# Second layer's product by one level of Strassen's algorithm, with operands of the second batch and the residual kept in HBM

## What is computed

```python
def _L0_xattn_ref(x1, x2, x1_scale, x1_zp, x2_scale, x2_zp):
    q1 = fake_quant(x1, x1_scale, x1_zp)      # clip(round(x / s + z), 0, 255), then (q - z) * s
    q2 = fake_quant(x2, x2_scale, x2_zp)
    return jnp.matmul(q1, q2)

def _L0_ffn_ref(x, W_base, b_base, W_router, lora_A, lora_B):
    logits = xf @ W_router.T
    probs = jax.nn.softmax(logits, axis=-1)
    topk_p, topk_i = jax.lax.top_k(probs, TOP_K)            # 2 of 8 experts
    topk_p = topk_p / jnp.sum(topk_p, axis=-1, keepdims=True)
    w = jnp.sum(jax.nn.one_hot(topk_i, n_experts, dtype=xf.dtype) * topk_p[..., None], axis=1)
    h = jnp.einsum('td,erd->ter', xf, lora_A)
    lora_out = jnp.einsum('ter,eor,te->to', h, lora_B, w) * SCALING
    base = x @ W_base.T + b_base
    return base + lora_out.reshape(x.shape[:-1] + (W_base.shape[0],))

x = x + _L0_xattn_ref(_layernorm(x, axis=-1), ctx_4096, ...)
x = x + _L0_ffn_ref(_layernorm(x, axis=-1), ...)
```

## Time and profile before

| | |
|---|---|
| median of 3 runs | 1059.66 us (1059.44 to 1062.93) |
| span of the profiled execution, first to last instruction | 1055.8 us |
| PE busy | 1007.5 us, 95% of the span |
| DVE, ACT, POOL busy | 565.6, 306.6, 295.8 us |
| HBM read, written | 97.00 MB, 17.83 MB |

### The profile page before, as it was taken

The page is one execution under the profiler, slowest core; times in us unless marked ns, Lnnn a source line. Parts: engine busy times, 40 slices in busy tenths (PEclk is TensorE's granted clock), DMA queues, the critical chain, the costliest instruction groups (busy, mean ns, idle before and its releaser), DMA issues.

```text
span 1055.8 us, 12263 instructions
## 1 busy us (share of the span) xinstructions
PE 1007.5 (95%) x4828; PEld 469.5 (44%) x4850; DVE 565.6 (54%) x693; ACT 306.6 (29%) x286; POOL 295.8 (28%) x215
## 2 busy tenths in 40 slices
...
GB/s 332 327 303 315 285 221 312 196 205 223 83 43 63 63 63 63 60 63 63 47 37 63 20 63 59 44 63 20 63 53 51 63 20 63 87 100 63 63 21 40
DMA packets 26702, 115.68 MB, mean 110 GB/s; under 512 B 3216, under 2 KB 6288, under 8 KB 19216
## 3 DMA queue, kind: packets, MB, share of 16 engines
q1 hardware_dynamic: 26640, 114.84, 29.8%
...
HBM read 97.00 MB, written 17.83 MB: 109 GB/s over the span
## 4 chain that ended last, share of the span: by engine, by line
PE 74%; issue 12%; DVE 7%; POOL 5%; ACT 2%; DMA 0%; POOLq 0%; DVEq 0%; ACTq 0%
PE PS L609 21%; PE PS L611 20%; PE PS L613 20%; PE PS L376 7%; DVE X L473 1%; DVE S L467 1%; PE PS L633 1%; PE PS L631 1%; PE PS L632 1%; POOL mv L276 1%; DVE S L404 1%; DVE X L427 1%; POOL mv L275 1%; POOL mv L279 1%; PE PS L410 1%
## 5 line engine op out<-in xcount | busy, mean ns | idle before, releaser
L609 PE MATMUL PS<-X,S 128*128 128x512 f16 x1088 | 326.7, 379 | 7.9 <-DVE Bs L578 5.4
L611 PE MATMUL PS<-X,S 128*128 128x512 f16 x1088 | 326.5, 379 | 0.0
L613 PE MATMUL PS<-X,S 128*128 128x512 f16 x1088 | 326.3, 379 | 0.0
L664 DVE SCALAR_TENSOR_TENSOR Q<-PS,wc,Q 128x512 f32<-128x512 f32 x64 | 45.2, 746 | 272.3 <-PE PS L633 272.3
L609 PEld LDWEIGHTS PS<-X,S 128*128 128x128 f16 x1088 | 105.9, 100 | 133.1 <-DVE Bs L578 9.3
L613 PEld LDWEIGHTS PS<-X,S 128*128 128x128 f16 x1088 | 106.5, 98 | 128.7 <-issue 0.5
L611 PEld LDWEIGHTS PS<-X,S 128*128 128x128 f16 x1088 | 106.4, 98 | 128.8 <-issue 0.6
L573 ACT ACTIVATE S<-S,wc 128x2048 f16<-128x2048 f32 x23 | 46.0, 2001 | 310.0 <-DVE wc L568 310.0
L500 POOL TENSOR_TENSOR wc<-wc,cst 128x1 f32<-128x1 f32 x25 | 14.8, 591 | 418.8 <-DVE wc L499 418.8
L376 PE MATMUL PS<-Q,S 128*128 128x512 bf16 x501 | 111.0, 379 | 0.7
L376 PE MATMUL PS<-X,S 128*128 128x512 bf16 (+1 forms) x502 | 105.6, 368 | 4.3 <-DVE st L272 2.0
...
## 6 DMA issues: line engine op xcount, KB each, us to landing
S<-in_cT_dram SPq DMA_DIRECT2D x32, 1024.0 KB, 6.3
S<-in_wT_dram SPq DMA_DIRECT2D x23, 1024.0 KB, 5.8
X<-in_xT_dram SPq DMA_DIRECT2D x32, 512.0 KB, 7.9
out_dram<-Q SPq DMA_DIRECT2D x31, 512.0 KB, 3.0
X<-in_xn_dram SPq DMA_DIRECT2D x20, 512.0 KB, 7.8
S<-in_xn_dram SPq DMA_DIRECT2D x12, 512.0 KB, 6.7
S<-in_aT_dram SPq DMA_DIRECT2D x2, 1024.0 KB, 5.2
Braw<-in_bT_dram SPq DMA_DIRECT2D x23, 64.0 KB, 5.5
```

The costliest lines, as they stand in the source:

```text
L609: e.matmul(bank(2 * p + h), ws[:, 0, 128 * k:128 * (k + 1)], xh(b, k, h), start=(k == 0), stop=False)
L611: e.matmul(bank(2 * p + h), ws[:, 0, 128 * k:128 * (k + 1)], xl(b, k, h), start=False, stop=False)
L613: ins = e.matmul(bank(2 * p + h), ws[:, 1, 128 * k:128 * (k + 1)], xh(b, k, h), start=False, stop=(k == KT - 1 and not lora))
L664: t = dve.do([out_of[n, b], ob_in[j]], lambda e, v=v, h=h: e.scalar_tensor_tensor(v, bank(2 * p + h), wc[n % 2][:, 7:8], v, op0=ALU.mult, ...
```

## The change

The weights' rows are taken in pairs of row tiles (256 outputs), the features in two halves of 1024 and the tokens in two halves of 512. One level of Strassen's algorithm (Winograd's form) makes the four quarter products of such a pair out of seven instead of eight. Per batch and row pair there are 7 products of 8 steps of 3 matmuls (128 x 512), and 4 tails of 3 for the low-rank term.

- The seven operands of the activations (`B11, T1, B21, B22, T2, T3, T4`: quarters, and sums and differences of them) are made by `y_operands`, each split into float16 high part and rest. For batch 0 they fill the 16 tiles `XA` and an area `EX`. For batch 1 they are made one eighth at a time, stored to HBM (`yd`) and loaded by `y_load` into the same places as batch 0's last group sets them free.
- The seven operands of the weights are made in each group: `w_scaled` scales four pieces in place (ACT), `w_sum` makes four sums (DVE), `w_hi` (ACT) and `w_lo` (DVE, three of seven on POOL) split them.
- The first layer's tiles are stored to HBM (`keep`). The residual comes back from there (`ob_load`), so `x_again` and the two maps are gone. Batch 1's tiles have only two staging buffers; its second norm loads them again (`tile_load`), centres them, stores them (`cd`) and loads them a third time (`ln_load`).
- The order in the second layer is written as times in `Plan`: a start for each of 16 groups, and offsets from it. `Plan` counts in strips `g`; `us(t)` is a place t microseconds behind the end of the first layer (32 + t / 6.92). These numbers only sort the lists.
- The weights' power-of-two scale is found once per row pair, in the first batch's groups only.

```diff
-        P.at(g - 0.95 if g > 3 else 2.6, ctx_conv, g, dve if g < 24 else pool)
+        P.at(g - 0.95 if g > 3 else 2.6, ctx_conv, g, dve if g < 19 else act)
+        P.at(g + 1.2 + (g < NT) * 0.4, keep, g)
...
+    def keep(g):
+        w = [keep_out[g - 4]] if g >= 4 else []
+        keep_out[g] = sp.do(w + [x2_ready[g]], sl_keep[g % 4], kept[g // NT, g % NT], xt(g))
+        if g >= NT:
+            stage_free[g % 2] = stage_free[g % 2] + [keep_out[g]]
...
+    def add1(nt):
+        t = stage[nt % 2]
+        if nt == 0:
+            sums[1] = [act.do([x2_ready[NT]], lambda e: e.activation(acc1, t, ACT.Copy, bias=0.0, scale=1.0))]
+        else:
+            sums[1] = [pool.do(sums[1] + [x2_ready[NT + nt]], lambda e: e.tensor_tensor(acc1, acc1, t, ALU.add))]
+        stage_free[nt % 2] = list(sums[1])
...
+    def centre1(i):
+        y = dve.do([misc["mean"], tile_in[i]], lambda e: e.tensor_tensor(v, v, bank(6, 2), ALU.subtract))
+        out = sp.do([y], sl_cd[s], cd[i], v)
+            sq = act.do([y] + sq_free[s], lambda e: e.activation(sq1[s], v, ACT.Square))
+            sums[1] = [pool.do(sums[1] + [sq], lambda e: e.tensor_tensor(acc1, acc1, sq1[s], ALU.add))]
+        tile_free[s] = [sq, out]
...
+    def y_operands(b, k):
+        A, B, TX = lnA[b], lnB[b], lnT[b]
+        scaled = lambda dst, src, w: dve.do([misc["r"]] + w, lambda e: e.tensor_tensor(dst, src, bank(6, 2), ALU.mult))
+        diff = lambda dst, x, y, w, line=dve: line.do(w, lambda e: e.tensor_tensor(dst, x, y, ALU.subtract))
+        high = lambda dst, src, w: act.do(w, lambda e: e.activation(dst, src, ACT.Copy, bias=0.0, scale=1.0))
+        a = scaled(A, srcA, wA)
+        c = scaled(B, srcB, wB)
+        hb = high(hB, two(B), [c] + wh[1])
+        t3 = diff(TX[:, 512:1024], B[:, 512:1024], A[:, 512:1024], [a, c] + ([] if b else ln_free["T"]))
+        t1 = diff(A[:, 512:1024], A[:, 512:1024], A[:, 0:512], [t3])
+        ha = high(hA, two(A), [t1] + wh[0])
+        t2 = diff(TX[:, 0:512], B[:, 512:1024], A[:, 512:1024], [t1])
+        ht = high(hT, two(TX), [t2] + wh[2])
+        yield
+        la = diff(lA, two(A), hA, [ha])
+        t4 = diff(A[:, 512:1024], B[:, 0:512], TX[:, 0:512], [la, t2])
+        h_4 = high(h4, A[:, 512:1024], [t4] + wh[3])
+        lb = diff(lB, two(B), hB, [hb, t4])
+        yield
+        lt = diff(lT, two(TX), hT, [ht, t4], pool if LT_POOL else dve)
+        l_4 = diff(l4, A[:, 512:1024], h4, [h_4])
+        if b:
+            ... eight stores to yd, in rows of 256 words
...
+    def y_load(op):
+        w = sum((v if isinstance(v, list) else [v] for v in yd_out.values()), [])
+        t = sp.do(w + [op_free[op]], sl_yl[op], yall(op), yd[op])
...
+    OPS = (B11, T1, T2, B21, B22, T3, T4)
+    BANK = (0, 2, 1, 0, 2, 1, 1)
+    def product(i, n, k0=0, k1=8):
+        op, bk = OPS[n], 3 * (i % 2) + BANK[n]
+            for k in range(k0, k1):
+                e.matmul(bank(bk), wh[:, c], yh(op, k), start=(fresh and k == 0), stop=False, skip_group_check=not fresh)
+                e.matmul(bank(bk), wh[:, c], yl(op, k), start=False, stop=False, skip_group_check=not fresh)
+                ins = e.matmul(bank(bk), wl[:, c], yh(op, k), start=False, stop=(fresh and k == 7), skip_group_check=not fresh)
+            w = w + wtok + (bank_free[bk] if fresh else evac_done[i, {3: 0, 4: 1, 5: 2, 6: 5}[n]])
...
+    start = [32 + 38.4 * i for i in range(8)]
+    start += [start[7] + 38.4 + 25 + 38.4 * i for i in range(8)]
+    y_at = lambda k: NT + 8.0 + 1.5 * k
+        for f, u in enumerate((0, 0.75, 1.2)):
+            P.at(y_at(k) + u, lambda o=o: next(o))
...
+    for k in range(8):
+        t = 118 + 22.5 * k
+        P.at(us(t - 5), ln_load, k)
+        o = y_operands(1, k)
+        for f, u in enumerate((0, 5, 8)):
+            P.at(us(t + u), lambda o=o: next(o))
...
+        P.at(us(t - 18), raw_load, i % 8)
+            for u in (-11, -7.9, -7.4, -6.8):
+                P.at(us(t + u), lambda o=o: next(o))
+        for u, q in ((-6, (0,)), (-5, (2, 3)), (-2, (1,))):
+            P.at(us(t + u), w_scaled, i, q)
+            u = t - 4.8 + 3 * n
+            P.at(us(u - 1.3), w_sum, i, n)
+            P.at(us(u), w_hi, i, n)
+            P.at(us(u + 1.2), w_lo, i, n, pool if n in (3, 5, 6) else dve)
+        at = [5.12 * n for n in range(6)] + [33.3]
+        for n, u in ((2, 30.8), (0, 31.5), (1, 32.2), (3, 38.35)):
+            P.at(us(t + u), tail, i, n)
+        for n, u in ((0, 5.2), (1, 10.3), (2, 15.4), (5, 31.6), (3, 32.3), (4, 33.1), (6, 38.5)):
+            P.at(us(t + u), post, i, n)
```

More of the change, by code:

```diff
@@ new lines, in mean, with centre0 @@
+    def mean(b):
+        misc["mean"] = ones(acc1 if b else acc0, sums[b], mean_w)
+        sums[b] = []
+        for q in sq_free:
+            q.append(misc["mean"])
+    def centre0(i):
+        v = XA[:, i, :]
+        y = dve.do([misc["mean"]], lambda e: e.tensor_tensor(v, v, bank(6, 2), ALU.subtract))
+        bank_free[6] = bank_free[7] = [y]
+        if i < 2:
+            a = (acc0, accD)[i]
+            sq_of[i] = act.do([y, misc["mean"]], lambda e: e.activation(a, v, ACT.Square))
+        else:
+            sq_of[i] = act.do([y] + sq_free[i % 2], lambda e: e.activation(sq0[i % 2], v, ACT.Square))
@@ new lines, in xattn_lora_ffn, with router, mm @@
+    h_wait, g_ready = {}, {}
+    def router(b):
+        bk = 6 if b else 4
+        lg = gexp = gsw
+        hb = hbuf[b]
+        left = [(B11, 0), (B21, 8)]
+        right = [(T1, 0), (B11, 0), (B22, 8)]
+        def mm(e):
+            for h, parts in enumerate((left, right)):
+                todo = [(op, k, k + k0) for op, k0 in parts for k in range(8)]
+                n = len(todo) // 4
+                for r, yy in ((r_a, yh), (r_b, yl)):
+                    for q in range(n):
+                        for g in range(4):
+                            op, k, kr = todo[4 * q + g]
+                            ins = e.matmul(bank(bk + h)[32 * g:32 * (g + 1), :], r[:, kr, :], yy(op, k),
+                                           start=(q == 0 and r is r_a), stop=(q == n - 1 and r is r_b), skip_group_check=True)
+            return ins
+        t = pe.do(once["r"] + bank_free[bk] + bank_free[bk + 1] + sum((opr[op, k] for op in (B11, T1, B21, B22) for k in range(8)), []), mm)
+        t = act.do([t] + ([once["tail"]] if b else []) + stage_free[0] + stage_free[1], lambda e: e.activation(lg, bank(bk, 2), ACT.Copy, bias=0.0, scale=1.0))
@@ L818, in xattn_lora_ffn @@
         P.at(lead(45 + 1.7 * g), evac1, g, 1)
+        P.at(lead(52 + 1.7 * g), keep, g)
     P.at(4, more_constants)
@@ L835, in xattn_lora_ffn @@
         P.at(t + 1.45, ln1_back, 1, i, 0, act)
-    adds, mean, centres, var_a, var_b, scales = ln2(0)
     for nt in range(1, NT):
-        P.at(max(nt + 1.2, 3.4), adds[nt - 1])
-    P.at(NT + 0.8, mean)
-    for i in range(NT + 1):
-        P.at(NT + 1.1 + 0.42 * i, centres[i])
-        P.at(NT + 9.3 + 0.45 * i, scales[i])
-    P.at(NT + 8.3, var_a)
-    P.at(NT + 8.9, var_b)
-    ahead = steps(early(), 7)
-    for t in (18, 20.5, 22.3, 22.7, 23.4, 24.3, 25.6):
-        P.at(t, ahead.pop(0))
@@ new lines, in xattn_lora_ffn, with first_raw, first_ring, first_done @@
+    o = early()
+    for t in (16.6, 18.5, 19.3, 19.7, 20.4, 21.3, 22.6):
+        P.at(t, lambda o=o: next(o))
+    us = lambda t: 2 * NT + t / 6.92
+    def first_raw():
+        raw_free[0], raw_free[1] = list(ctx_free[0]), list(ctx_free[1])
+        raw_load("A", (0,))
+        raw_load(0, (1,))
+    def first_ring():
+        ring_free[0] = sum(u8_free, []) + misc["acc_read"]
+        ring_free[1] = list(ring_free[0])
+        a_prep(0)
+    def first_done():
+        q = once["q_done"] = half_done[2 * NT - 1, 1]
+        for s in range(2, NR):
+            ring_free[s] = [q]
+        wt_free[0], wt_free[1] = [q], [q]
+        ob_free[0], ob_free[1] = [q], [q]
+        h_wait[0] = [q]
+        r_prep()
```

798 lines of the change are left out of this document (440 added, 358 removed).

## The result

The changed kernel takes 1148.78 us (median of 4 runs, 1146.55 to 1149.76), the kernel before 1060.72 beside it: ratio 1.082, 95% interval 1.080 to 1.084. It is slower; 1015 was forecast.

What follows compares the result with a forecast made beforehand. PE's matmul count bounds it. From 1055.8, 83.1 removed work and 10.7 old losses came off; router 2 and further terms 7, 14, 13, 5, 3, 1, 4 were added: 1011, with 3.9 around the span 1015 us; range 982 to 1050.

Steps and rivals of the forecast that it cites:

- first layer, first half: First layer's first half: `keep` adds DMA traffic beyond full rate, prefetch covers a little; +4 us (0 to 10).
- first layer, second half: First layer, g = 24 to 32: DVE's eighths, evacuations and POOL additions make PE wait; +7 us (0 to 20).
- between the layers: From the end of `gemm1` to product 0: PE waits for the last eighths and weights' sums; +14 us (6 to 25).
- groups 0 to 7: Second layer, batch 0: DVE waits beside batch 1's norm 9 us, bank waits at product 6 4; +13 (4 to 35).
- between the batches: Change of batch: 20 MB queued on the DMA, the weights last and still to be scaled; +5 us (2 to 20).
- groups 8 to 15: Second layer, batch 1, with no norm beside the groups; +3 us (0 to 10).
- sign of a lower time: Second layer, groups 2 to 7: idle time on DVE there would show that the forecast was wrong low.
- Removed work: Second layer's products: 2688 matmuls in place of 3072, at 0.2165 us each; -83.1 us.
- Transfers through HBM slow at y_load: Rival, at `y_load`: slow HBM transfers make the kernel slower, 1087 us at 150 GB/s; 0.09, shared with several stalls.
- DVE becomes the bound: Rival: in-order lists couple everything, three DVE terms of 20, 25 and 30 us give 1056; 1035 to 1054 had 0.13.
- Waits mostly hidden: Rival, whole kernel: POOL, DVE and ACT's waits overlap, low ends of the terms hold, 980 to 1000 us; chance 0.27.

Runs made afterwards that it cites:

- e4: The changed kernel without batch 1's norm, groups 8 to 15 computing with batch 0's operands: 1041.8 us.
- e5: The changed kernel without the transfers of batch 1's norm, its arithmetic kept in place: 1104.6 us.
- e9: The changed kernel with the weights' scale of group 0 used for all groups, no squares, scale matmul or power for groups 1 to 7: 1122.7 us.
- e13: The changed kernel without the norm's transfers and without the weights' scale of groups 1 to 7, the norm's arithmetic kept: 1068.7 us.
- e6: The changed kernel without the POOL additions of batch 1's norm, all transfers and POOL's three rests per group kept: 1137.3 us.
- e15: The changed kernel without the norm's transfers, the weights' scale of groups 1 to 7 and the norm's POOL additions: 1059.7 us.
- run 896: Not a follow-up run: "run" is a verb here, three source lines of product matmuls execute 896 times each, 2688 in all.

## Why the prediction was wrong

Stretch by stretch, what was forecast and what was measured:

| stretch | forecast, us over PE's work | measured |
|---|---|---|
| first layer, first half | 4 | 0 |
| first layer, second half | 7 | 27 |
| between the layers | 14 | 31.6 |
| groups 0 to 7 | 13 | 119.2 |
| between the batches | 5 | 7.6 |
| groups 8 to 15 | 3 | 10.9 |

The rows miss by 150 us together and the span by 137 (1147.9 against 1011): the forecast also carried some 13 us that the kernel before spends in its second layer outside 300 to 500 us on waits and small matmuls.

**The step that failed** is *Groups 0 to 7*: it left 9 us for batch 1's norm beside these groups, where e4 shows 107.0. It priced the norm by the busy time of DVE, and called its cycles through HBM hidden ("some 17 with queueing, against 22.5 in the list") and the centring "I count nothing, up to 8". In the trace an eighth starts every 29 us (L551, two in each eighth, 1.2 apart, from 512.7 to 717.3: 203.4 / 7) and a tile every 7.0 (L490, (482.2 - 376.7) / 15). Each cycle is load, DVE, ACT, store, next load, each link in a queue with other work; without any transfer e5 still has 5.5 per tile where the list has 4. When one is late, the engine waits with the posts and the next weights' sums queued behind it, and PE pays at L620 or at a product. That what DVE "waits for at a `post` PE pays at the next weights" was right; 2 us a group for it was not, nor 35 as the high end. (The sum there is also misadded, 29.8 + 4.7 to 6 + 4 is 38.5 to 39.8, which changes little.) Its sign of a lower time, idle DVE in groups 2 to 7, was there, and the time was higher. That transfers and scale each hold PE, and by some 8 us hide each other, is shown by e5, e9 and e13; the POOL additions' 8 to 16 us by e6 and e15. Not settled: which link would have to be cut with nothing left out (longer periods, a third buffer and another queue did not do it).

**Not counted at all** was the clock: matmuls at 1.2 GHz behind the waits, some 24 us in groups 0 to 7 and most of the 31.4 - 25.7 = 5.7 between the layers.

**Removed work** was right: L775 to L777 run 896 times each, 2688 in all, and from 850 to 900 us, undisturbed, PE is busy throughout. **First half**: `keep` cost nothing; the last matmul of batch 0's strips starts at 154.6 us, and at 154.8 in the kernel before. **Second half**: gemm1 ends at 299.7 us against 272.4. DVE is full as forecast (57.85 of 64 us from 236 to 300), but the price was near 27, not 7; waits of 13.6 for ACT's conversions behind `ha` and 6.7 for the variance (L508) are 20.3 of it, and some 4 more are matmuls at half pace. **Between the layers** PE's waits are these, 25.9 in all with L861's two:

```profile
PE PS L620 <- DVE WC L685: 9.2, 1, 9.2
PE PS L861 <- DVE S L426: 8.1, 1, 8.1
...
PE PS L775 <- ACT Q L812: 5.7, 1, 5.7
PE PS L903 <- DVE Q L880: 2.3, 1, 2.3
PE PS L861 <- DVE XA L552: 0.6, 1, 0.6
```

The waits for L426 and L552 were in the forecast, and L685 lies on the path that it priced, behind ACT's squares of the first weights; but the last part of `lora_h`, behind it on PE, starts 38.5 us after `gemm1` in place of 29.7. Not in the forecast was the wait ahead of the first product. It is for the operand's `w_lo` (L741) and not for L812: ACT had scaled the quarter for it by 344.5 us, but has its `w_hi` (L736) in the list behind the router's copy (L907), which waits for the router:

```profile
351.29 1.02 ACT L907 ACTIVATE S<-PS 128x1024 f32<-128x1024 f32 x1 [6.83 <-PE PS L903]
352.21 2.17 ACT L705 ACTIVATE S<-S,WC 128x1024 f32<-128x1024 f32 x2
354.29 1.04 ACT L736 ACTIVATE Q<-S 128x1024 f16<-128x1024 f32 x1
```
```profile
355.37 1.23 DVE L741 TENSOR_TENSOR Q<-S,Q 128x1024 f16<-128x1024 f32 x1 [10.62 <-ACT Q L736]
```

**Between the batches** the size was near and the reason wrong: PE waits 5.6 us for the first operand in the same way (L741 ends at 821.0 us, the product starts at 821.3) and 2.3 for the evacuation of `lora_h` (L880), and not for a transfer.

**The rivals.** *Transfers through HBM slow at y_load* came out on the right side by the wrong mechanism. The loads ran at full share:

```profile
750.00:800.00 50.00, 48.55 (x226) 21.85 (x225) 14.94 (x16) 8.29 (x8) 6.34 (x3) 1.00 0.96 361
```

The rule of the Trainium skill (DMA: Bandwidth & Descriptors, Specifications) that 512 bytes are the least transfer for full rate agrees with it: these rows are 2 KB, the rate 361 GB/s. *DVE becomes the bound* named in-order coupling ("a late `post` is a late product") but kept DVE busy as its price; DVE is at 59% in these groups. *Waits mostly hidden* fails on e4 already, which has no norm and takes 1041.8 in place of 980 to 1000.
